# Scores of four heads in one go in the first attention of a four-layer network

## The reference, cut to what matters

```python
B, S, T, H, HD = 8, 112, 375, 16, 128; KVC, QC, R = 128, 192, 64
kv_c = kv @ W_kvc                                  # 375 x 128, the same for all heads
k_rope, q_rope = rope(kv_c @ W_kr), rope(q_c @ W_qr)   # 64 wide
scores = (einsum('bhqd,bkhd->bhqk', q_nope, k_nope)
          + einsum('bhqr,bkr->bhqk', q_rope, k_rope)) * scale
scores = where((k_ids <= seg_id) & (k_ids >= seg_id - 8), scores, -1e30)
attn = softmax(scores)
out = einsum('bhqk,bkhd->bqhd', attn, v).reshape(b, lq, H * HD) @ W_o
x = x + tanh(g_xattn[0]) * out
```

## Time and profile before

| | value |
|---|---|
| median of three executions | 2694.35 us |
| profiled execution / its span | 2697.19 / 2695.4 us |
| TensorE busy over the span | 2415.3 us (90%) |
| one of the four head groups, from its first scores to the next group's first weight matmul | 222.71 to 319.73 us |
| one step of the pipeline within it | 11.52 us |
| granted TensorE clock, mean of the span | 0.933 |

### The profile page before, as it was taken

One profiled execution on the slowest core, in us unless ns is written; L12 is line 12 of the kernel. 1 busy time (PEld: TensorE's weight loads), 2 busy tenths in 40 slices (PEclk: granted clock), 3 DMA queues, 4 the chain that ended last, 5 costly groups with the idle time before them and its releaser, 6 DMA issues. The chain is left out here.

```text
span 2695.4 us, 35390 instructions
## 1 busy us (share of the span) xinstructions
PE 2415.3 (90%) x10421; PEld 1433.8 (53%) x10422; DVE 999.0 (37%) x2413; ACT 651.3 (24%) x1467; POOL 453.7 (17%) x607
## 2 busy tenths in 40 slices
PE   7899998988888898888889999875999999889888
PEld 4444444454664656656546555442665665345476
DVE  5535344443325234143622223561222222612375
ACT  2444353620111234143201110110111111051221
POOL 6000000003112000000141113316111111700061
PEclk9999999988998998998889999767999999989999
DMA  9101000032772000000516664250444542551220
GB/s 374 57 1 32 24 8 0 0 107 83 246 236 82 20 6 13 17 6 1 156 48 198 201 196 123 83 157 13 145 144 132 160 159 87 160 204 48 82 82 28
DMA packets 151929, 263.96 MB, mean 98 GB/s; under 512 B 16406, under 2 KB 80510, under 8 KB 151325
## 3 DMA queue, kind: packets, MB, share of 16 engines
q1 hardware_dynamic: 117789, 186.08, 21.3%
q0 software_dynamic: 19072, 49.35, 6.5%
q10 hardware_dynamic: 14976, 27.27, 2.7%
HBM read 212.77 MB, written 49.88 MB: 97 GB/s over the span
## 5 line engine op out<-in xcount | busy, mean ns | idle before, releaser
L360 POOL DMA_INDIRECT slot_list<-token_ids,slots x64 | 62.0, 969 | 618.5 <-DVEq L546 599.6
L924 PE MATMUL bank<-f2r_wd,f2b_hT 128*128 (+1 forms) x300 | 137.2, 593 | 1.4 <-DVE f2b_hT L1028 1.4
L250 PE MATMUL bank<-ident,xn 112*128 112x112 f32 x256 | 59.1, 397 | 86.0 <-DVE xn L226 86.0
L905 PE MATMUL bank<-f2r_wg,f2b_xT 128*128 x400 | 128.9, 466 | 1.4 <-ACT f2b_xT L961 1.1
L905 PE MATMUL bank<-f2r_wu,f2b_xT 128*128 x400 | 126.5, 460 | 0.0
L1355 PE MATMUL bank<-l0a_vo,l0a_zT 128*112 128x512 f32 x256 | 115.5, 594 | 2.9 <-DVE l0a_zT L1513 2.9
L1325 PE MATMUL bank<-l_kvcT,xnT 128*112 128x375 f32 x256 | 98.0, 507 | 20.7 <-DVE l0a_qrT L1485 20.7
L360 POOL DMA_INDIRECT slot_list<-token_ids,slots_in x32 | 31.2, 974 | 501.1 <-DVEq L546 492.0
L1416 ACT ACTIVATE l0a_p<-l0a_p,l0a_low 112x375 f32<-112x375 f32 x128 | 77.1, 607 | 114.8 <-DVE l0a_low L1506 113.6
L1015 DVE TENSOR_TENSOR f2b_h<-bank,f2b_acted 128x352 f32<-128x352 f32 x50 | 26.2, 524 | 205.9 <-PE bank L905 205.9
L1496 DVE CUSTOM_DVE_ANT_0 l0a_p<-bank,xn 112x375 f32<-112x375 f32 x128 | 70.3, 549 | 83.2 <-PE bank L1327 83.2
(11 more groups left out here) (375 smaller groups left out, 4551.2 us busy)
## 6 DMA issues: line engine op xcount, KB each, us to landing
slot_rows<-zeros SPq DMA_DIRECT2D x2, 7424.0 KB
slot_rows<-f2b_y ACTq DMA_DIRECT2D x50, 256.0 KB, 3.8
f1r_wg<-in_l_wg SPq DMA_DIRECT2D x16, 704.0 KB, 4.5
f1r_wu<-in_l_wu SPq DMA_DIRECT2D x16, 704.0 KB, 6.2
f2r_wg<-in_l_wg SPq DMA_DIRECT2D x16, 704.0 KB, 4.5
f2r_wu<-in_l_wu SPq DMA_DIRECT2D x16, 704.0 KB, 6.4
xn<-in_l_w_ffn SPq DMA_DIRECT2D x11, 768.0 KB, 4.3
l_raw<-in_l_w_ffn SPq DMA_DIRECT2D x11, 768.0 KB, 4.4
```

The source lines that it names most:

```text
L250: mm = pe.transpose(s.bank[n % 4][:, k * TOK:(k + 1) * TOK], s.xn[:, n, k * 128:(k + 1) * 128], s.ident[0:TOK, 0:TOK])
L360: pool.indirect_dma_start(s.slot_list, bass.IndirectOffsetOnAxis(ap=slots[:, k, b:b + 1], axis=0), s.token_ids[:, b:b + 1], None, **bound) ...
L905: mm = pe.matmul(bank[:, 0:width], xT[:, v, k, :], w[:, bass.ds(at, 1), k, :].rearrange("p o f -> p (o f)"), start=(k == 0), stop=(k == KD ...
L924: mm = pe.matmul(bank_y[v][:, :], hT[0:fn, v, c, :], wd[0:fn, bass.ds(at, 1), c, :].rearrange("p o f -> p (o f)"), start=(c == 0), stop=(c ...
```

## The change

TensorE does the scores of all four heads of a batch at once: the eight 128-row matmuls, then the eight 64-row tails. The four turns of the batch before follow the mix without scores between them. ScalarE and VectorE are put in the matching order: ScalarE does exponentials 0 and 1, the four copies of turned weights, exponentials 2 and 3, and then the four normalizations; VectorE does four masks, the copy of the mix, and then the four reciprocals. The wait ahead of scores is one wait for the masks of all four heads of the batch before, where there were two waits for two heads each.

```diff
-            def scores(g, b, pair):
+            def scores(g, b):
                 toks, keys = slice(b * TOK, (b + 1) * TOK), slice(b * T, (b + 1) * T)
-                heads = (2 * pair, 2 * pair + 1)
                 if b:
-                    pe.wait_ge(s_masked, 1 + g * N + (b - 1) * GH + 2 * pair + 2)
-                for j in heads:
+                    pe.wait_ge(s_masked, 1 + g * N + b * GH)
+                for j in range(GH):
                     pe.matmul(s.bank[j][0:TOK, 0:T], qT[:, j, toks], a.kvcT[:, keys], start=True, stop=False)
-                for j in heads:
-                    pe.matmul(s.bank[j][0:TOK, 0:T], qrT[row_group(j), pair, toks], a.krT[row_group(j), keys],
+                for j in range(GH):
+                    pe.matmul(s.bank[j][0:TOK, 0:T], qrT[row_group(j), j // 2, toks], a.krT[row_group(j), keys],
                               start=False, stop=True).then_inc(s_done, 1)
...
                     if n < B:
-                        scores(g, n, 0)
+                        scores(g, n)
                     if 0 <= n - 2:
                         mix(g, n - 2)
                     if 0 <= n - 1 < B:
-                        turn(g, n - 1, 0)
-                        turn(g, n - 1, 1)
-                    if n < B:
-                        scores(g, n, 1)
-                    if 0 <= n - 1 < B:
-                        turn(g, n - 1, 2)
-                        turn(g, n - 1, 3)
+                        for j in range(GH):
+                            turn(g, n - 1, j)
                     if 0 <= n - 2:
                         project(g, n - 2)
...
                         exponential(g, n, 0)
                         exponential(g, n, 1)
-                        normalize(g, n, 0)
-                        normalize(g, n, 1)
                     if n:
                         for j in range(GH):
                             copy_turned(g, n - 1, j)
                     if n < B:
                         exponential(g, n, 2)
                         exponential(g, n, 3)
-                        normalize(g, n, 2)
-                        normalize(g, n, 3)
+                        for j in range(GH):
+                            normalize(g, n, j)
...
-                    for pair in range(2):
-                        if n < B:
-                            for j in (2 * pair, 2 * pair + 1):
-                                mask(g, n, j)
-                                shift_of(g, n, j)
-                            for j in (2 * pair, 2 * pair + 1):
-                                invert(g, n, j)
-                        if pair == 0 and 0 <= n - 2 < B:
-                            copy_mix(g, n - 2)
+                    if n < B:
+                        for j in range(GH):
+                            mask(g, n, j)
+                            shift_of(g, n, j)
+                    if 0 <= n - 2 < B:
+                        copy_mix(g, n - 2)
+                    if n < B:
+                        for j in range(GH):
+                            invert(g, n, j)
```

## The result

Five executions of the changed kernel took 2708.55 to 2717.41 us, median 2715.18; those of the kernel before, in the same job, 2687.25 to 2698.57, median 2694.32. The ratio is 1.0076, 95% interval 1.0053 to 1.0098: slower by 20.9 us. The forecast was 2709.3 us, range 2701 to 2720. The profiled execution took 2716.03 us, its span 2714.3, 18.9 more than before. One execution of the kernel before, in the job of the last experiments, took 4974.73 us and is left out of the ratios.

What follows compares the result with a forecast made beforehand. TensorE's own list was taken to bound the steady state; +5.8 us from steady steps and +9.2 from group starts gave +15.0, from a median of 2694.35 to 2709.3 us, range 2701 to 2720.

Steps and rivals of the forecast that it cites:

- TensorE's own list sets the time in the steady state, and a step gets 0.24 us longer: Steps 2 to 7 of each group: TensorE always busy, a step 11.76 against 11.52 us, +5.8 us in all.
- the block of tails: In each step's scores: one block of tails costs about 0.4 us beyond its work, saved when two are joined.
- the uncovered copy: Ahead of the third turn in each step: ScalarE's copy, no longer hidden by scores, costs 0.64 us, at least 0.38.
- The others are in time: Steady steps: ScalarE and VectorE keep up, the first copy with 1.2 us to spare; SyncE, GpSimd and DMAs cost nil.
- Rival 2: ScalarE late with the first copy in every step, third turn 0.3 us later in 24 steps: +7, 2716.5 us; chance 0.05.
- The start of a group costs 2.3 us: Steps 0 and 1: second scores wait for the mask, third turn for its copy; +2.3 us a group, +9.2 in all.
- Sum +15.0 us: Whole kernel: +5.8 us from steady steps and +9.2 from group starts, median 2694.35 to 2709.3 us.
- Rival 1: Start of each group: TensorE's clock falls in the new wait, +8.6 us, 2717.9 us; chance 0.22.
- The price of 2.15: Start of each group: a clock fall lasting 4.3 us costs 2.15 us a group.
- Rival 3: Steps and starts: saved tails decide, the copy doesn't hold up the third turn, so not slower; chance 0.11.
- its 24 x 0.40: Steady steps: with no wait for the copy, 24 steps save 0.40 us each, 9.6 us in all.
- a rule for tiled matmuls: Four turns: a skill page says tiling speeds TensorE but not PSUM's emptying, so the copy can limit; cited for 1.92 us.

Runs made afterwards that it cites:

- e6: Changed kernel with the scores ordered full 0 1, tails 0 1, full 2 3, tails 2 3; ratio to the kernel before 1.0059, 18.5 us slower by medians.
- e3: Changed kernel with TensorE's mix moved between turns 0, 1 and turns 2, 3; ratio to the kernel before 1.0038, 11.6 us slower by medians.
- e1: Changed kernel with steps 0 and 1 of each head group in the old order by pairs; ratio to the kernel before 1.0013.
- e2: Changed kernel with steps 2 to 9 in the old order by pairs, steps 0 and 1 by fours; ratio to the kernel before 1.0033.
- e4: e3 with the pairs of e1 in steps 0 and 1; ratio to the kernel before 0.9981, 6.2 us faster by medians.
- e5: Changed kernel with ScalarE copying the four turns ahead of exponentials 0 and 1 in step 1 alone; ratio to the kernel before 1.0046.
- e7: Kernel before with four more 512-column products on TensorE at each head group's start, a pure delay; ratio to the kernel before 1.0046.
- e9: Changed kernel, steps 0 and 1 by pairs, then mix, turns 0 and 1, scores, turns 2 and 3, project; ratio to the kernel before 0.9999.

## Why the prediction was right

- *TensorE's own list sets the time in the steady state, and a step gets 0.24 us longer.* Right: 11.77 against 11.53. Both terms behind it were borne out separately: the block of tails at 0.38 (e6; forecast 0.4), the uncovered copy by e3, where it vanished once something stood between the turns. Step 2 showed a wait of 0.30, later steps 0.38.
- *The others are in time.* Right: besides the turns' copies and the start, TensorE has no new wait in the view of waits. Rival 2 did not occur.
- *The start of a group costs 2.3 us.* Right: 2.1 to 2.4, mean 2.27 (sum 9.1, forecast 9.2), by the wait for the mask (2.25, forecast 2.4) and the copy behind the exponentials. e1 removed it, e2 kept it alone.
- *Sum +15.0 us.* The stage gave 14.7. The whole gave 20.9, 18.6 and 17.7 by medians in three jobs (ratios 1.0076, 1.0078, 1.0062). The step that fell short is the tacit one, that everything outside the stage keeps its duration: the router took 3.3 us more, at half clock, in all three profiles. That these 3.3 recur, and that e1 and e4 gained 3.3 there, is shown. That the end time of the stage sets them is not: the changed kernel's last projection started at 580.0 and 583.4 us, and in e3, e5 and e7 it started between these two, at 580.3 to 581.4, yet their router kept the 21.9 us of before. What is left, up to 3 us, is within the scatter. So the mechanism and the sum of the stage were right, while the total, 5.9 us above the forecast, lies in the range by its allowance for scatter and for a fall of the clock at another place, which is partly luck.
- *Rival 1, the clock falls in the new wait.* Not in the changed kernel, but in e2, e3 and e5, with the same wait of 2.25 us, at 1.7 to 2.8 us a time. Its chance of 0.22 was not too high. The price of 2.15 took the 4.3 us at half clock behind the first scores for the whole stretch; the fall itself stood for 3.4 us and cost 1.7.
- *Rival 3, not slower.* Refuted by the 0.38 ahead of the third turn; e9 shows that with all copies covered the steps do gain 0.39, as its 24 x 0.40 said. The prediction also explained the 1.92 us of the four turns by a rule for tiled matmuls, but the turns are not tiled (112*125 in their rows). What holds the third turn is ScalarE's copy out of the bank that it shares with the first.

## What to carry to other kernels

When instructions are moved together to save a switch, ask what they stood between: here the second half of the scores hid 0.56 to 0.64 us of waiting for a copy, worth more than the 0.4 us of the switch. Look for a place in the trace that already runs the new order (here the last step of the pipeline, and the preparation with its four tails in a row) and take the price from there, and sum up the first steps of each loop by themselves: they cost 9 of the 15 us. Behind a stage whose end moves, expect some us either way from TensorE's clock, and don't credit them to the order.

## What the runs showed of the hardware

- A wait of TensorE of the same length (2.25 us) left the clock at full in all twelve groups of the three changed profiles, and was followed by half clock in five of the twelve groups of e2, e3 and e5. In those five the clock had stood at half for 5.4 us or more from the first scores on (6.2 in e3's group 1, 226.77 to 232.93), in the others for 5.1 or less (4.3 to 4.7 in the changed kernel). The length of the wait alone doesn't tell, and what does is not shown.
- The same 38 matmuls of the router took 18.6, 21.9 or 25.2 us (from the first one's start to that of the next after them), depending on whether the clock was at half for none of it, for 6.8 or for 13.7 us.
- Two pairs of 64-row matmuls in different row halves ran side by side at the same pace however many followed: 1.45 us for four heads, 0.82 for two, so 0.63 for each further pair of heads.
